# Where the step size of a selective scan is assembled: VectorE, or ScalarE and GpSimd

## The chip, the cores and the metric

The kernel runs on one core of a Trainium2 chip. The metric is the device time of one execution in microseconds (us). The core has four compute engines that this document names: PE (TensorE, matmuls), DVE (VectorE), ACT (ScalarE) and POOL (GpSimd); SP (SyncE) issues the DMA transfers. Each engine takes its own list of instructions in order and waits on semaphores where the list says so.

## The reference

Two layers run one after the other on x of shape 2 x 2048 x 512, all in float32. The first is a selective scan (Mamba) block with adaptive layer norm, the second a linear attention block. The change touches the first layer alone, and in it the step size `dt`:

```python
dt = jax.nn.softplus(einsum('bsr,dr->bsd', dt_r, dt_proj_w) + dt_proj_b)
A = -exp(A_log)                                     # 1024 x 16
def step(h, inp):                                   # over 2048 positions
    dt_t, B_t, C_t, u_t = inp
    dA = exp(dt_t[:, :, None] * A)
    h = h * dA + (dt_t * u_t)[:, :, None] * B_t[:, None, :]
    y = einsum('bdn,bn->bd', h, C_t)
    return (h, y)
y = (y + u * D_param) * silu(z)                     # then out_proj, gate, residual
```

softplus(x) is computed as max(x, 0) + ln(1 + exp(-|x|)). So `dt` is the sum of a rectified part, max(x, 0), and a logarithm.

## The kernel before

The 2 x 2048 positions are cut into 8 chunks (`c`) of 512 positions, and the 1024 channels into 8 blocks (`j`) of 128. One chunk and one block make a unit, `U = 8 * c + j`, so there are 64 units. A unit has 16 slots (`pr`), one for each state index n; `s = 16 * U + pr` counts slots over the program (1024 of them). Two slots form a group `G` (8 per unit), whose 128 x 1024 tile `hb[G % 6]` is one of six buffers. What each engine does for a unit:

- ACT: `softplus(U)` makes `Abs` of the product in PSUM, then `Exp`, then `Ln` in place in the tile `spt`; `exps(s)` writes dA for slot s into one of four PSUM banks (`DA`), three slots ahead of the scan that reads it; `du_copy` copies dt * u into the bank `DU`. ACT also evacuates the projections of the next chunk (`x_evac`, seven ACTIVATEs and sometimes an eighth), applies silu, and copies the end states (`keep_state`). Silu needs another activation table than exp and ln, so each visit to silu has a table load ahead of it and one behind it (L748 by `preload_act_table_set`); silus that share a slot share the two loads.
- DVE: `add(U)` (L933) reads PSUM and `spt` and writes `dt`; `expand(G)` (L943) makes dt * u * B for two state indices; `scan(s)` (L955) runs the recurrence over 512 positions; `y_fin(U)` (L961) multiplies by silu(z).
- POOL: `du(U)` (L1310) makes dt * u; then for each group one multiplication by C of 128 x 1024 (L1339). In the slots of the table `HALF` POOL also adds the two halves of the group (L1344), which saves PE one of two matmuls. POOL adds three taps of the convolution for each of 8 blocks of the next chunk (L1304), and computes the layer norm's small factors (`neg_means` L1297, `rs2` L1288 to L1292), and in chunks 0 and 4 gates the output weights (`gate_w`, L1315).
- PE: sums the 16 states of a unit into PSUM by matmuls with the identity (`nsum`, L299 for the D term, L303 for the groups), and does the projections: `x_mm`, `z_mm` (L250), `proj` (L276), `dt_mm` (L283), `out_mm` (L289).

Waiting between engines: a scan waits for its dA from ACT and its expanded group; ACT's `exps(s)` waits for scan s - 4; POOL's multiplication waits for the group's two scans and, where `kept(U)` holds, for ACT's copy of its end states; `expand(G)` waits until PE has summed group G - 6; `y_fin` of a unit's predecessor waits for its last sum.

The order of the work is written out by hand: at each slot, every engine's loop looks whether `(j, pr)` stands in a table. `AT` holds slots that recur in each unit (`dt`, `soft`, `add`, `du`, `copy`, `yf`), the others (`XMM`, `SILU`, `ZMM`, `STATS`, `RS1`, `SQ`, `RS`, `NORM`, `NTR`, `NEV`, `OUTM`, `OUTA`, `HALF`, `GATE`) slots of a chunk. `XEV` and `TAP` follow from `XMM`. Since each engine takes its list in order, a slot early in one list can come later in time than a later slot of another.

Of the kernel before, what the change touches and what calls it, by code (L numbers as in the profile page):

```python
# [18 lines left out]
def program(nc, A, out):  # L19
# [12 lines left out]
    with ctx:  # L32
        def sem(name):
            return ctx.enter_context(nc.semaphore(name))
# [126 lines left out]
        STATS = {(0, 4): 0, (1, 0): 1}
        RS1 = {(0, 0): 0, (1, 1): 1}
        SQ = {(0, 6): 0, (1, 7): 1}
        RS = {(0, 4): 0, (1, 5): 1}
        NORM = {(0, 8): 0, (1, 10): 1}
        NTR = {(0, 13): 0, (2, 1): 1}
        NEV = {(1, 0): 0, (2, 2): 1}

        OUTM = {(0, 4): 0, (0, 7): 4, (1, 2): 8, (1, 5): 12, (2, 3): 16, (2, 4): 20, (2, 8): 24, (2, 10): 28}
        OUTA = {(0, 9): 0, (1, 9): 1, (2, 8): 2, (3, 0): 3}  # L170
# [1487 lines left out]
```

## Time and profile before

| | |
|---|---|
| time, median of 3 runs | 2452.96 us (2450.15 to 2453.13) |
| profiled execution | 2451.58 us, of which the instructions span 2449.8 us |
| PE busy | 2223.1 us (91%) |
| DVE busy | 2199.2 us (90%) |
| ACT busy | 1618.9 us (66%) |
| POOL busy | 1858.9 us (76%) |
| first scan starts, last scan starts | 81.4 us, 1950.9 us |

The span has three stretches: a start of 81 us, the scan loop of the first layer up to about 1952 us, and the second layer. In the slices of the page DVE stands at 90% or more from the second slice of the scan loop to its end, and POOL and PE at 80% to 90%. The table's shares are means over all three stretches. The chunks are told apart by the start of each one's first scan: 81.4, 322.1, 556.0, 789.2, 1022.0, 1250.4, 1485.5 and 1718.2 us.

### The profile page before, as it was taken

How to read it: one execution, taken by the hardware profiler on the slowest of the kernel's cores; microseconds unless marked ns; L12 is line 12 of the kernel's file. 1: busy time of each engine (PE TensorE's matmuls, PEld its weight loads, DVE VectorE, ACT ScalarE, POOL GpSimd, SP SyncE). 2: the span in 40 equal slices, each digit the busy share in tenths (PEclk: the TensorE clock that was granted, in tenths of full speed). 3: DMA queues.
4: the chain of work that ended last, by engine and by line, in shares of the span. 5: the costliest groups of instructions: out<-in, count | busy, mean ns of one | idle time of the engine just before them, and what ended most of it. 6: DMA issues, size and time to landing. Idle time of an engine off the chain costs nothing. (4 is left out here: it accounts for less than half of the span.)

```text
span 2449.8 us, 24055 instructions
## 1 busy us (share of the span) xinstructions
PE 2223.1 (91%) x6900; PEld 1152.6 (47%) x6900; DVE 2199.2 (90%) x2424; ACT 1618.9 (66%) x3175; POOL 1858.9 (76%) x1205
## 2 busy tenths in 40 slices
PE   8788999899988998898989889988887899999989
PEld 3233334333333433343334333433333389988878
DVE  3799999999999999999999999999999966666656
ACT  3667877777777777777867777777555455466655
POOL 0499989998999899889989998999887722222225
PEclk9899999999999999999999999999998999999999
DMA  5610141123104110412041114112200220011113
GB/s 196 228 57 26 39 156 43 30 97 102 39 26 159 44 35 26 156 52 65 22 177 39 31 47 145 33 30 104 86 31 1 84 76 29 29 57 57 48 52 121
DMA packets 78050, 176.10 MB, mean 72 GB/s; under 512 B 7453, under 2 KB 10781, under 8 KB 77918
## 3 DMA queue, kind: packets, MB, share of 16 engines
q1 hardware_dynamic: 77918, 174.56, 21.5%
q8 instruction: 56, 0.92, 0.2%
q14 instruction: 76, 0.62, 0.1%
HBM read 157.23 MB, written 17.30 MB: 71 GB/s over the span
## 5 line engine op out<-in xcount | busy, mean ns | idle before, releaser
L955 DVE TENSOR_TENSOR_SCAN arena<-ps,arena 128x512 f32<-128x512 f32 x1024 | 1248.9, 1248 | 3.2 <-ACT ps L541 3.2
L1339 POOL TENSOR_TENSOR arena<-arena 128x1024 f32<-128x1024 f32 x512 | 1200.2, 2357 | 65.0 <-ACT arena L541 44.3
L541 ACT ACTIVATE ps<-arena 128x512 f32<-128x512 f32 x1088 | 729.2, 683 | 436.2 <-DVE arena L955 409.8
L303 PE MATMUL ps<-arena,keep 128*128 128x512 f32 x1736 | 840.9, 616 | 104.2 <-POOL arena L1339 57.9
L943 DVE TENSOR_TENSOR arena<-ps,arena 128x1024 f32<-128x1024 f32 x512 | 612.2, 1196 | 22.2 <-PE ps L303 11.6
L303 PEld LDWEIGHTS ps<-arena,keep 128*128 128x128 f32 x1736 | 327.4, 195 | 570.7 <-issue 346.6
L250 PE MATMUL ps<-arena 128*128 128x512 f32 x1024 | 476.2, 610 | 4.6 <-ACT arena L541 3.0
L250 PEld LDWEIGHTS ps<-arena 128*128 128x128 f32 x1024 | 200.7, 197 | 266.4 <-issue 263.2
L541 ACT ACTIVATE arena<-arena 128x2 f32<-128x2 f32 (+2 forms) x597 | 228.8, 386 | 26.4 <-DMA arena<-in_x 10.1
L289 PE MATMUL ps<-arena 128*128 128x512 f32 x512 | 231.3, 592 | 0.0
L1304 POOL TENSOR_TENSOR arena<-arena 128x512 f32<-128x512 f32 x168 | 213.6, 1271 | 9.6 <-ACT arena L541 3.2
L1344 POOL TENSOR_TENSOR arena<-arena 128x512 f32<-128x512 f32 x156 | 197.9, 1268 | 12.2
L541 ACT ACTIVATE arena<-ps,keep 128x509 f32<-128x509 f32 (+3 forms) x240 | 168.6, 703 | 50.3 <-PE ps L250 38.7
L1310 POOL TENSOR_TENSOR arena<-arena 128x512 f32<-128x512 f32 x64 | 81.3, 1271 | 109.9 <-DVE arena L933 109.9
L1357 POOL TENSOR_TENSOR arena_c<-arena_c 128x512 f32<-128x512 f32 x32 | 33.4, 1044 | 167.2 <-DVE arena_c L1104 166.1
L541 ACT ACTIVATE arena<-ps 128x512 f32<-128x512 f32 (+2 forms) x209 | 100.5, 494 | 82.7 <-PE ps L289 27.1
L289 PEld LDWEIGHTS ps<-arena 128*128 128x128 f32 x512 | 97.2, 190 | 122.8 <-issue 122.4
L299 PE MATMUL ps<-arena 128*128 128x512 f32 x128 | 76.1, 679 | 86.0 <-DVE arena L961 85.7
L1271 POOL TENSOR_SCALAR arena_b<-arena_b 128x2 f32<-128x2 f32 x32 | 8.2, 257 | 156.4 <-DVE arena_b L1053 156.4
L541 ACT ACTIVATE arena_b<-ps,keep 128x256 f32<-128x256 f32 x128 | 70.9, 554 | 52.8 <-PE ps L406 43.3
L541 ACT ACTIVATE arena_c<-arena_c 128x256 f32<-128x256 f32 (+3 forms) x112 | 54.9, 493 | 74.6 <-POOL arena_c L1357 47.6
L1064 DVE TENSOR_TENSOR xl<-arena_b,xh 128x256 fp32r<-128x256 f32 x128 | 57.6, 467 | 41.9 <-ACT xh L541 41.1
(138 smaller groups left out, 2567.4 us busy)
## 6 DMA issues: line engine op xcount, KB each, us to landing
arena<-scr_bc SPq DMA_DIRECT2D x128, 512.0 KB, 6.7
arena<-in_inT SPq DMA_DIRECT2D x128, 256.0 KB, 2.7
arena<-in_x SPq DMA_DIRECT2D x17, 512.0 KB, 3.8
scr_x<-arena SPq DMA_DIRECT2D x32, 256.0 KB, 2.0
arena_b<-scr_x SPq DMA_DIRECT2D x16, 512.0 KB, 3.8
arena_c<-scr_x SPq DMA_DIRECT2D x32, 256.0 KB, 2.9
out<-arena_c SPq DMA_DIRECT2D x32, 256.0 KB, 2.0
arena<-in_x SPq DMA_DIRECT2D x30, 256.0 KB, 3.8
```

The costliest lines, as they stand in the source:

```text
L250: last = e.matmul(P, W[:, q, :], xnT[c % 2][:, q, :], start=(q == 0), stop=(q == 3))
L289: e.matmul(P, u[c % 2][:, q, 128 * n:128 * n + 128], wout[:, q, :], start=(c == NCH - 1 and q == 0 or parts and q == 6), stop=(q == 7 or p ...
L299: e.matmul(YP, dg[U % 2], u[c % 2][:, j, :], start=True, stop=False)
L303: last = e.matmul(YP, ident, hb[G % R][:, i, :], start=False, stop=(g == NG - 1 and i == n - 1))
L541: return e.activation(o_, i_, f, **kw)
L943: e.tensor_tensor(hb[G % R], DU.unsqueeze(1).broadcast_to([128, GN, T]), Bt[:, GN * g:GN * g + GN, :], MUL).then_inc(v_tt)
L955: e.tensor_tensor_scan(H, DA[s % 4], H, h0, MUL, ADD).then_inc(v_sc)
L1064: e.tensor_tensor(lo[:, f, :], f_bufs[i % 3], hi[:, f, :].bitcast(f32), SUB).then_inc(v_lo)
L1304: e.tensor_tensor(v, v, tp[:, w, :], ADD).then_inc(g_tap)
L1310: e.tensor_tensor(spt, dt[U % 2], u[c % 2][:, j, :], MUL).then_inc(g_du)
L1339: m_ = e.tensor_tensor(H, H, Ct[:, GN * g:GN * g + GN, :], MUL)
L1344: m_ = e.tensor_tensor(H[:, 0, :], H[:, 0, :], H[:, 1, :], ADD)
```

## The change

In each of the 64 units, DVE's instruction that takes the maximum with zero and adds the logarithm is gone. ACT takes the rectified part from PSUM in a new `Relu` ACTIVATE between `Exp` and `Ln`, and POOL adds `spt` to it in place with a new TENSOR_TENSOR of 128 x 512, ahead of `du`. ACT's exponentials and POOL's `du` now wait for POOL's addition (`g_dt`) where they waited for DVE's (`v_dt`), and the PSUM bank of the product is released by the `Relu`. The tables are written anew; `HALF` has 18 entries in place of 20 a chunk.

```diff
-        AT = {"dt": 4, "soft": 7, "add": 8, "du": 7, "copy": 13, "yf": 7, "proj": (6, 15), "xdbl": (7, 2)}
-        XMM = {(2, 14): 0, (3, 4): 1, (4, 0): 2, (4, 4): 3, (4, 12): 4, (5, 1): 5, (6, 1): 6, (6, 7): 7}
+        AT = {"dt": 5, "soft": 7, "add": 6, "du": 7, "copy": 12, "yf": 6, "proj": (6, 15), "xdbl": (7, 2)}
+        XMM = {(3, 0): 0, (3, 6): 1, (4, 2): 2, (4, 10): 3, (4, 13): 4, (5, 0): 5, (5, 14): 6, (6, 7): 7}
...
-        SILU = {(3, 14): (0, 2), (5, 14): (2, 5), (6, 15): (5, 8)}
+        SILU = {(4, 3): (0, 2), (5, 9): (2, 5), (6, 15): (5, 8)}
...
-        HALF = {0: (5, 7), 1: (1, 3, 7), 2: (0, 2, 3, 4, 5), 3: (0, 2), 4: (3, 4), 5: (3,), 6: (5,), 7: (0, 2, 3, 4)}
+        HALF = {0: (2, 5, 6), 1: (2, 3, 6), 2: (1, 2, 3, 4), 3: (0,), 4: (0,), 5: (), 6: (5,), 7: (0, 3, 4, 5, 7)}
...
-                P = bank(("dt", U), (v_dt, U + 1))
+                P = bank(("dt", U), (a_rl, U + 1))
...
                 e.wait_ge(a_ex, U + 1)
+
+                if U >= 2:
+                    e.wait_ge(g_du, U - 1)
+                act(dt[U % 2], BG[bank_of["dt", U]], ACT.Relu).then_inc(a_rl)
                 act(spt, spt, ACT.Ln, bias=1.0).then_inc(a_ln)
...
-            def add(U):
-                e.wait_ge(a_ln, U + 1)
-                if U >= 2:
-                    e.wait_ge(a_da, 16 * (U - 1))
-                e.scalar_tensor_tensor(dt[U % 2], BG[bank_of["dt", U]], 0.0, spt, MAX, ADD).then_inc(v_dt)
...
+            def add(U):
+                e.wait_ge(a_ln, U + 1)
+                e.tensor_tensor(dt[U % 2], dt[U % 2], spt, ADD).then_inc(g_dt)
+
             def du(U):
                 c, j = divmod(U, 8)
-                e.wait_ge(v_dt, U + 1)
+                e.wait_ge(g_dt, U + 1)
...
+                if U + 1 < NU and pr == AT["add"]:
+                    add(U + 1)
                 if U + 1 < NU and pr == AT["du"]:
                     du(U + 1)
```

On POOL, in unit 0 (chunk 0), before: L1310 is `du`, L1339 the multiplication by C, L1297 `neg_means`, L1288 to L1292 `rs2`, L1344 the halves. The rows begin with `du` of unit 0.

```order
L1310 TENSOR_TENSOR arena<-arena 128x512
L1297 TENSOR_SCALAR arena<-arena 128x2
L1339 TENSOR_TENSOR arena<-arena 128x1024 x2
L1288 TENSOR_SCALAR arena<-arena 128x2
L1290 TENSOR_TENSOR arena<-arena,keep 128x2
L1292 TENSOR_TENSOR arena<-arena 128x2
L1339 TENSOR_TENSOR arena<-arena 128x1024
L1310 TENSOR_TENSOR arena<-arena 128x512
```

The same place now (the lines are those of the changed file: L1303 is the new `add`, L1309 `du`, L1341 the multiplication, L1346 the halves, L1292 `neg_means`, L1283 to L1287 `rs2`).

```order
L1309 TENSOR_TENSOR arena<-arena 128x512
L1341 TENSOR_TENSOR arena<-arena 128x1024 x2
L1292 TENSOR_SCALAR arena<-arena 128x2
L1341 TENSOR_TENSOR arena<-arena 128x1024
L1346 TENSOR_TENSOR arena<-arena 128x512
L1283 TENSOR_SCALAR arena<-arena 128x2
L1285 TENSOR_TENSOR arena<-arena,keep 128x2
L1287 TENSOR_TENSOR arena<-arena 128x2
L1303 TENSOR_TENSOR arena<-arena 128x512
L1309 TENSOR_TENSOR arena<-arena 128x512
```

`neg_means` stood ahead of the unit's first multiplication and stands behind its second. A TENSOR_TENSOR of 128 x 512 is new right ahead of `du`, both still ahead of the unit's fourth multiplication.

On ACT, in unit 5 of a chunk, now: softplus (four rows that alternate between `arena<-ps` and `arena<-arena`), then four rows of exponentials and end states, and a visit to silu with a pair of table loads of its own. Before, that silu of 128 x 1536 stood with the silu of z in slot (5, 14).

```order
L541 ACTIVATE arena<-ps 128x512
L541 ACTIVATE arena<-arena 128x512
L541 ACTIVATE arena<-ps 128x512
L541 ACTIVATE arena<-arena 128x512
L541 ACTIVATE ps<-arena 128x512 x2
L541 ACTIVATE arena<-arena 128x2
L541 ACT_TABLE_LOAD
L541 ACTIVATE arena<-arena 128x1536
L752 ACT_TABLE_LOAD
L541 ACTIVATE ps<-arena 128x512 x2
```

Over the whole program ACT's list has 123 table loads in place of 95 (four more in each of chunks 0 to 6) and 64 more ACTIVATEs `arena<-ps`; POOL's has 64 additions more and 139 halves in place of 156; PE's has 885 matmuls at L303 in place of 868.

## Rows read from the trace of the kernel before

**Rows 1.** Windows, one per chunk: stretch, length, then each engine's busy time
```profile
81.40:322.10 240.70, 208.48 (x466) 81.78 (x467) 230.31 (x216) 170.60 (x347) 221.32 (x127) 0.93 0.27 92
322.10:556.00 233.90, 213.15 (x483) 89.52 (x481) 232.57 (x209) 171.83 (x351) 216.82 (x125) 0.98 0.21 67
556.00:789.20 233.20, 210.96 (x481) 89.33 (x480) 232.57 (x209) 171.18 (x343) 216.14 (x125) 0.98 0.20 68
789.20:1022.00 232.80, 210.35 (x481) 88.94 (x480) 232.53 (x210) 165.41 (x289) 216.00 (x125) 0.99 0.21 68
1022.00:1250.40 228.40, 208.83 (x480) 89.06 (x480) 225.02 (x210) 169.42 (x347) 215.36 (x123) 0.99 0.23 76
1250.40:1485.50 235.10, 214.33 (x490) 91.24 (x489) 232.82 (x210) 173.23 (x352) 220.71 (x127) 0.98 0.22 70
1485.50:1718.20 232.70, 210.54 (x481) 88.70 (x480) 232.49 (x210) 171.44 (x343) 216.02 (x125) 0.99 0.20 66
1718.20:1952.10 233.90, 194.06 (x412) 81.85 (x412) 231.16 (x209) 119.74 (x181) 183.48 (x92) 0.91 0.14 49
```

**Rows 2.** Groups of DVE by line: busy us, mean ns | idle before, releasers
```profile
L955 DVE TENSOR_TENSOR_SCAN arena<-ps,arena 128x512 f32<-128x512 f32 x1024 | 1248.9, 1248 | 3.2 <-ACT ps L541 3.2
L943 DVE TENSOR_TENSOR arena<-ps,arena 128x1024 f32<-128x1024 f32 x512 | 612.2, 1196 | 22.2 <-PE ps L303 11.6 <-ACT ps L541 8.2 <-DMA arena<-scr_bc 2.3
...
L933 DVE SCALAR_TENSOR_TENSOR arena<-ps,arena 128x512 f32<-128x512 f32 x64 | 42.3, 661 | 9.7 <-ACT arena L541 9.7
```

**Rows 3.** Timeline of DVE around one `add`: start, us, instruction
```profile
570.54 1.27 DVE L955 TENSOR_TENSOR_SCAN arena<-ps,arena 128x512 f32<-128x512 f32 x1
571.73 0.66 DVE L933 SCALAR_TENSOR_TENSOR arena<-ps,arena 128x512 f32<-128x512 f32 x1
572.31 1.27 DVE L955 TENSOR_TENSOR_SCAN arena<-ps,arena 128x512 f32<-128x512 f32 x1
```

**Rows 4.** Timeline of DVE at the start of the loop
```profile
76.70 1.22 DVE L943 TENSOR_TENSOR arena<-ps,arena 128x1024 f32<-128x1024 f32 x1 [2.01 <-ACT ps L541]
80.25 1.23 DVE L943 TENSOR_TENSOR arena<-ps,arena 128x1024 f32<-128x1024 f32 x1 [2.33 <-DMA arena<-scr_bc]
```

**Rows 5.** The page's costliest groups: POOL and PE
```profile
L1339 POOL TENSOR_TENSOR arena<-arena 128x1024 f32<-128x1024 f32 x512 | 1200.2, 2357 | 65.0 <-ACT arena L541 44.3
...
L303 PE MATMUL ps<-arena,keep 128*128 128x512 f32 x1736 | 840.9, 616 | 104.2 <-POOL arena L1339 57.9
...
L1344 POOL TENSOR_TENSOR arena<-arena 128x512 f32<-128x512 f32 x156 | 197.9, 1268 | 12.2
...
L1310 POOL TENSOR_TENSOR arena<-arena 128x512 f32<-128x512 f32 x64 | 81.3, 1271 | 109.9 <-DVE arena L933 109.9
```

**Rows 6.** Waits in chunk 2: us in total, times, longest
```profile
POOL arena L1339 <- ACT arena L541: 7.2, 5, 3.6
...
POOL arena L1310 <- DVE arena L933: 3.7, 3, 1.6
...
POOL arena L1297 <- ACT arena L541: 2.9, 1, 2.9
```

**Rows 7.** Waits of POOL in chunk 0
```profile
POOL arena L1297 <- ACT arena L541: 12.0, 1, 12.0
```

**Rows 8.** Timeline of ACT in chunk 2: a visit to silu, and softplus
```profile
666.60 0.69 ACT L541 ACTIVATE ps<-arena 128x512 f32<-128x512 f32 x1 [0.59 <-DVE arena L955]
667.31 1.28 ACT L541 ACT_TABLE_LOAD   x1
668.60 1.08 ACT L541 ACTIVATE arena<-ps 128x512 f32<-128x512 f32 x2
...
683.27 0.59 ACT L541 ACTIVATE arena<-ps 128x512 f32<-128x512 f32 x1
683.89 1.29 ACT L541 ACTIVATE arena<-arena 128x512 f32<-128x512 f32 x2
685.09 0.68 ACT L541 ACTIVATE ps<-arena 128x512 f32<-128x512 f32 x1
```

**Rows 9.** The page's costliest groups: ACT's exponentials
```profile
L541 ACT ACTIVATE ps<-arena 128x512 f32<-128x512 f32 x1088 | 729.2, 683 | 436.2 <-DVE arena L955 409.8
```

More of the change, by code:

```diff
@@ L132, in program @@
             ("ft", "q", "v", "k", "qt", "kt", "kv", "ya", "o"))
-        a_sc, a_A, a_row, a_no, a_xn, a_xh, a_hi, a_tp, a_e0, a_du, a_su, a_xd, a_abs, a_ex, a_ln, a_sz, a_da, a_st, a_dg, a_x1, a_sm, a_sq = (
+        a_sc, a_A, a_row, a_no, a_xn, a_xh, a_hi, a_tp, a_e0, a_du, a_su, a_xd, a_abs, a_ex, a_ln, a_sz, a_da, a_st, a_dg, a_x1, a_sm, a_sq, a_rl = (
             sem("a_" + n) for n in ("sc", "A", "row", "no", "xn", "xh", "hist", "tp", "e0", "du", "su", "xd", "abs", "ex", "ln", "sz",
-                                    "da", "st", "dg", "x1", "sm", "sq"))
+                                    "da", "st", "dg", "x1", "sm", "sq", "rl"))
         a_wh, a_nx, a_f, a_fh, a_qe, a_qT, a_ek, a_E, a_fc = (sem("a_" + n) for n in ("wh", "nx", "f", "hi", "qe", "qT", "ek", "E", "fc"))
-        v_An, v_xe, v_st, v_ag, v_s1, v_tap, v_dt, v_tt, v_sc, v_yf, v_x1, v_xp, v_gb, v_ec, v_a2 = (
-            sem("v_" + n) for n in ("An", "xe", "st", "ag", "s1", "tap", "dt", "tt", "sc", "yf", "x1", "xp",
+        v_An, v_xe, v_st, v_ag, v_s1, v_tap, v_tt, v_sc, v_yf, v_x1, v_xp, v_gb, v_ec, v_a2 = (
+            sem("v_" + n) for n in ("An", "xe", "st", "ag", "s1", "tap", "tt", "sc", "yf", "x1", "xp",
                                     "gb", "ec", "a2"))
@@ L144, in program @@
                                     "att", "y", "o"))
-        g_c, g_r1, g_r2, g_r3, g_rs, g_nm, g_tap, g_du, g_gw, g_m, g_w = (sem("g_" + n) for n in ("c", "r1", "r2", "r3", "rs", "nm", "tap", "du", "gw", "m", "w"))
+        g_c, g_r1, g_r2, g_r3, g_rs, g_nm, g_tap, g_dt, g_du, g_gw, g_m, g_w = (sem("g_" + n) for n in ("c", "r1", "r2", "r3", "rs", "nm", "tap", "dt", "du", "gw", "m", "w"))
         g_att, g_m1, g_mask, g_l1, g_l2, g_lrs, g_q, g_xo = (sem("g_" + n) for n in ("att", "m1", "mask", "l1", "l2", "lrs", "q", "xo"))
@@ L154, in program @@
         XEV = {after(k, 4): i for k, i in XMM.items()}
         TAP = {after(k, (2, 3, 4)[w]): (i, 2 - w) for k, i in XMM.items() for w in range(3)}
-        SILU = {(3, 14): (0, 2), (5, 14): (2, 5), (6, 15): (5, 8)}
-        ZMM = {(1, 8): 1, (1, 10): 2, (3, 8): 1, (3, 10): 2, (5, 7): 1, (5, 11): 2, (7, 11): 1, (7, 12): 2}
+        SILU = {(4, 3): (0, 2), (5, 9): (2, 5), (6, 15): (5, 8)}
+        ZMM = {(1, 8): 1, (1, 10): 2, (3, 8): 1, (3, 11): 2, (5, 6): 1, (5, 10): 2, (7, 10): 1, (7, 13): 2}
@@ L159, in program @@
         ZSILU = {(1, 15): (1, 2), (3, 14): (1, 2), (5, 14): (1, 2), (7, 15): (1, 2)}
[L161 to L170, printed above, removed]
@@ L172, in program @@
-        HALF = {0: (5, 7), 1: (1, 3, 7), 2: (0, 2, 3, 4, 5), 3: (0, 2), 4: (3, 4), 5: (3,), 6: (5,), 7: (0, 2, 3, 4)}
+        STATS = {(0, 1): 0, (1, 2): 1}
+        RS1 = {(0, 3): 0, (1, 0): 1}
+        SQ = {(0, 7): 0, (1, 5): 1}
+        RS = {(0, 5): 0, (1, 5): 1}
+        NORM = {(0, 11): 0, (1, 12): 1}
+        NTR = {(0, 10): 0, (2, 0): 1}
+        NEV = {(0, 15): 0, (2, 1): 1}
+        OUTM = {(0, 9): 0, (0, 10): 4, (0, 14): 8, (1, 4): 12, (2, 2): 16, (2, 7): 20, (2, 10): 24, (2, 12): 28}
@@ L174, in program @@
+        OUTA = {(0, 14): 0, (1, 8): 1, (2, 11): 2, (3, 1): 3}
+        HALF = {0: (2, 5, 6), 1: (2, 3, 6), 2: (1, 2, 3, 4), 3: (0,), 4: (0,), 5: (), 6: (5,), 7: (0, 3, 4, 5, 7)}
         CPART = {after(k, n): (i, n) for i, k in enumerate([(0, 6), (1, 6), (2, 2)]) for n in range(4)}
         CROW, CCOL, CEND = {(0, 11): 0, (1, 11): 1, (2, 7): 2}, {(1, 14): 1, (2, 9): 2}, {(2, 1): 1, (2, 12): 2}
-        GATE = {(1, 8): (0, 0), (1, 12): (0, 1), (2, 0): (0, 2), (2, 4): (0, 3), (38, 14): (1, 0), (39, 3): (1, 1),
-                (39, 7): (1, 2), (39, 13): (1, 3)}
+        GATE = {(1, 10): (0, 0), (2, 15): (0, 1), (3, 13): (0, 2), (4, 14): (0, 3), (39, 1): (1, 0), (39, 6): (1, 1),
+                (39, 14): (1, 2), (39, 15): (1, 3)}
@@ L987, in _ @@
                 taps(i)
-            add(0)
             expand(0)
@@ L998, in _ @@
                 scan(s)
-                if U + 1 < NU and pr == AT["add"]:
-                    add(U + 1)
                 if (U, pr) in ((62, 14), (63, 4)):
@@ L1304, in tap @@
                 e.tensor_tensor(v, v, tp[:, w, :], ADD).then_inc(g_tap)
+            def add(U):
+                e.wait_ge(a_ln, U + 1)
+                e.tensor_tensor(dt[U % 2], dt[U % 2], spt, ADD).then_inc(g_dt)
             def du(U):
                 c, j = divmod(U, 8)
-                e.wait_ge(v_dt, U + 1)
+                e.wait_ge(g_dt, U + 1)
                 e.wait_ge(a_su, su_of(c))
@@ L1319, in _ @@
             rs(1)
+            add(0)
             du(0)
```

## Prediction, made before the changed kernel was run

> **What bounds the kernel now.** I read the windows by chunk first, then the groups by line of DVE and POOL, then the waits of POOL in one chunk, and last the timelines of DVE and ACT around the code that moves. The reader is to see in the windows [rows 1] that the scan loop is bound by DVE: in chunks 1, 2, 3 and 6 it is busy for 232.5 of about 233 us, while PE has 211 to 213, POOL 216 to 217 and ACT 165 to 172. The groups say the same from the other side: 1024 scans sat idle for 3.2 us in total and 512 expansions for 22.2 us [rows 2]. So time taken off DVE in the loop is time off the kernel, as long as no other engine stands close behind. POOL does: it has 216 us of work in a chunk of 233, an idle time of 17 us. That second number decides this case, because the change gives POOL more work and the chunk becomes shorter at the same time. The second layer and the start are as they were, apart from what is said of the first unit below.
>
> **The change part by part.** Sums are made against the profiled execution, 2451.58 us (span 2449.8 us and 1.8 us around it); it lies 1.4 us under the median of the runs, 2452.96 us, so the forecast holds for either within that.
>
> 1. *VectorE's addition goes.* It runs 64 times with a mean of 661 ns [rows 2], but instructions overlap a little: it starts at 571.73 and the next scan at 572.31 [rows 3], so it holds up the line for 0.58 us. 63 of them lie inside the loop: 63 x 0.58 = 36.5 us. In a chunk that is 8 x 0.58 = 4.6 us.
>
> 2. *The first unit.* Here the addition is on the path that starts the loop, and what replaces it is longer: a Relu before the logarithm (0.6 us, from the 0.59 us of Abs over the same shape and source [rows 8]) and 1.27 us of POOL, as du has it [rows 5], in place of 0.66 us. That is 0.6 + 1.27 - 0.66 = 1.2 us later for the first expansion. But the second expansion started only at 80.25, after waiting 2.33 us for the load of B [rows 4]. The delay is shorter than this wait, so I cost it at nothing; without the load as cover it is 1.2 us.
>
> 3. *POOL.* It gets 8 additions a chunk and loses 2 halves (20 entries in the table become 18), at 1.27 us each [rows 5]: +7.6 us a chunk (chunk 4, whose last unit takes no halves, loses 3: +6.4 us). Against the windows [rows 1], with DVE's length shortened by 4.6 us: chunk 2 has 223.7 us of POOL work in 228.6 us, chunks 3 and 6 have 223.6 in 228.1, chunk 1 has 224.4 in 229.3. What is left is 4.5 to 4.9 us of idle where there were 17.1 us (chunk 2). Of those 17.1 us, 7.2 were waits for ACT's copies of the end states, 3.7 for DVE's addition and 2.9 for row sums [rows 6], which leaves 3.3 us for the small gaps between dependent instructions. Those 3.3 us stay. So the waits, 13.8 us, must fall to about 1.3 us, or the chunk gets longer than DVE needs. I expect that most fall, for these waits are those of an engine that has caught up. With less slack POOL runs further behind DVE, and finds the thing it waits for already done. The wait for DVE's addition ends in any case: du stood at slot 7 and waited for an instruction that DVE issued behind scan 8; now POOL waits at slot 6 for ACT's logarithm, which ACT begins once scan 5 has let it issue exponential 9. Behind it in POOL's list stand du and the fourth multiplication, and for these wait ACT's next du_copy and PE's sum. I take 1 us of lost time for each of chunks 1 to 6, 6 us, between 0 and the bounds given under the rivals.
>
> 4. *Chunks 4 and 0.* Chunk 4 had 215.4 us of POOL in 228.4 [rows 1]; now 215.4 + 6.4 + 3.3 = 225.1 us in 228.4 - 4.6 = 223.8, and chunk 5 has 220.7 + 7.6 + 3.3 = 231.6 in 230.5. POOL is the longer one by 1.3 and 1.1 us. Such a shortfall can be carried on as a backlog, for six group buffers lie between the engines, and chunk 7, without taps, has POOL busy only 183.5 of 233.9 us; I add nothing beyond the 1 us each. In chunk 0 POOL waited 12.0 us for row sums at one place [rows 7]; `neg_means` now stands two multiplications later, and the gates are spread from units 1 and 2 to units 1 to 4. Its 10.4 us of DVE idle (240.7 less 230.3) should shrink; I take 2 us as a gain, between 0 and 6.
>
> 5. *ACT.* 64 Relus of 0.6 us are 38 us and 28 more table loads of 1.28 us [rows 8] are 36 us, together 74 us, or 10 us in each of seven chunks (and 5 in the eighth). ACT has 171 of 233 us in chunk 2, and waited for the scans for 409.8 us over the run before exponentials [rows 9], so the sum fits. What counts is the stretch: ACT is three exponentials ahead, some three scans and an expansion or two, about 5 us of cover. Softplus grows from 683.27 to 685.09, 1.8 us, to 2.4 us [rows 8]. Two visits to silu that shared a slot are now apart, each shorter than the joint one, so the longest block does not grow. I cost it at nothing; if the cover is gone, see the rivals.
>
> On the table loads the trace shows one that starts 0.02 us after the exponential before it ends and is followed by the silu 0.01 us after its own 1.28 us [rows 8]. The Trainium skill, ScalarE: Activation LUTs, "What ACT_TABLE_LOAD costs", gives the same 1283 ns but adds a drain of about 1380 ns for each switch; by that rule the 28 loads would be an estimated 75 us of ACT instead of 36, and the rival with ACT would be more likely. This case's trace does not show the drain.
>
> 6. *PE.* 17 more matmuls; 868 at L303 took 840.9 us [rows 5], so 0.97 us each, 2 us a chunk on top of 211 of 233. After the change 213 of 228, not the bound. Releasing the bank by the Relu instead of by DVE behind scan 8 can only help PE. Zero.
>
> Sum: -36.5 (1) + 0 (2) + 6 (3) - 2 (4) + 0 + 0 = -32.5 us. 2451.6 - 32.5 = 2419 us.
>
> **The rivals.**
>
> *A, DVE keeps its whole gain.* POOL's waits vanish, and the idle time of DVE in chunk 0 goes by up to 6 us. Then 2451.6 - 36.5 = 2415 us, down to 2409 us. For it: POOL's waits are short ones, and it had 17 us of idle in every chunk. Against: 4.5 us of slack less 3.3 us of fixed gaps is next to nothing.
>
> *B, POOL is the bound, moderately.* Of 17 us of idle about 6 stay (the gaps and one wait of 3 us). Then chunks 1, 2, 3 and 6 take 230.4, 229.7, 229.6 and 229.6 us, 13 us less than before together; chunks 4 and 5 take 227.8 and 234.3, 1.4 less; chunk 0 keeps the 4.6 us and chunk 7 too. -13 - 1.4 - 9.2 = -24, 2428 us. For it: the totals of rows 1. Against: a backlog can cover part.
>
> POOL takes 1.27 us for what DVE does in 0.66 [rows 2, 5]. The Trainium skill says in the GPSIMD Engine Reference, "Engine selection", that elementwise work belongs on VectorE and is about twice as slow on GpSimd for two inputs; the rows agree. It is a rule against this change, and B and D are what it would come to here.
>
> *C, ACT comes late.* In units 4 and 5 of a chunk the projections, the longer softplus and the lone silu stand close. If DVE waits there 2 to 3 us in each of chunks 0 to 6, 14 to 21 us come back: 2433 to 2440 us. For it: DVE waited for ACT even before, 8.2 and 3.2 us in total [rows 2]. Against: ACT's share of a chunk is only about 80% after the change.
>
> *D, slower.* The waits of POOL [rows 6] are not those of an engine that caught up but are set by ACT, and ACT is later now. Place: POOL's waits for the end states and for the logarithm, at slots 6 and 7 of each unit. A chunk is then POOL's work plus its idle time. Break-even: 233 - 216 - 7.6 = 9 us of idle a chunk; above it the kernel is slower. If 13 us stay, chunks 0 to 6 lengthen by 3.7 us each, 26 us, less 4.6 us for chunk 7: 2473 us. If all 17 stay, 54 - 5: 2500 us. Against it: POOL's waits are few and short (9 in chunk 2, the longest 3.6 us) [rows 6], which is how an engine waits that has caught up, not one that is held back each slot.
>
> That the change doesn't do what it says can be left out: the order of instructions shows no addition on DVE, and no table load between Exp, Relu and Ln.
>
> **How the numbers follow.** Forecast (POOL near full, DVE keeps nearly its pace, 2413 to 2424 us): 0.55. A: 0.13. B: 0.15. C: 0.11. D: 0.06. The range runs from 2411 to 2436 us: it takes in most of A and B and the lower half of C, and leaves out some 5 in 100 below and 11 above. A difference of 0.2% is about what a measurement can tell from none, 5 us; so faster is anything under 2448 us. All cases but D are faster; I keep 0.03 for a mixture that ends within 0.2%, and of D 0.04 for slower, the rest being in between: faster 0.93, same 0.03, slower 0.04.
>
> **What the new profile would show.** For the forecast: no L933-like row on DVE; chunks 1, 2, 3 and 6 at 228 to 230 us with DVE busy for 227 to 228; POOL busy 223 to 224 us in each and its waits for ACT down to a few us. For A: the same with DVE's waits under 0.5 us a chunk. For B: DVE's expansions or its final multiplications wait for PE, and PE for POOL, 1 to 3 us a chunk, with POOL's idle at 5 to 7 us. For C: waits of scans or expansions on ACT's exponentials, above all in units 4 and 5. For D: POOL's idle above 9 us and chunks longer than 233 us. The forecast is wrong at step 1 if DVE's busy time in a chunk doesn't fall by 4.6 us, at step 3 if POOL's work doesn't grow by 7.6 us or its waits stay, and at step 2 if the first scan starts later than 81.4 us.

## The result and the profile after

| | before | after |
|---|---|---|
| median of 4 runs each | 2452.8 us (2450.15 to 2453.13) | 2429.0 us (2427.4 to 2430.5) |
| ratio, 95% interval | | 0.9905 (0.9888 to 0.9922) |
| profiled execution | 2451.58 us | 2427.97 us |
| last scan ends | 1952.1 us | 1926.1 us |

The kernel is 23.8 us faster where 32.5 us were forecast; 2429 us lies inside the range from 2411 to 2436 us. Lines have moved: L953 is the scan, L941 the expansion, L959 `y_fin`, L1341 POOL's multiplication, L1346 the halves, L1299 the taps, L1303 the new addition, L1309 `du`.

These are the windows by chunk of the changed kernel: stretch, length, then busy time (and count) of PE, weight loads, DVE, ACT and POOL, the granted clock, and DMA. They answer to [rows 1].

```profile
81.70:322.70 241.00, 213.46 (x472) 81.32 (x472) 223.81 (x209) 179.82 (x359) 225.72 (x131) 0.94 0.26 91
322.70:552.40 229.70, 211.02 (x484) 88.92 (x484) 228.21 (x202) 179.94 (x363) 224.10 (x131) 0.99 0.21 71
552.40:782.10 229.70, 210.86 (x484) 88.92 (x484) 228.19 (x201) 179.23 (x355) 223.41 (x131) 0.99 0.21 68
782.10:1011.80 229.70, 211.97 (x484) 89.37 (x484) 228.21 (x201) 174.16 (x301) 223.45 (x131) 0.99 0.21 70
1011.80:1238.70 226.90, 209.18 (x485) 88.84 (x486) 221.00 (x201) 177.71 (x359) 223.07 (x129) 1.00 0.23 77
1238.70:1469.80 231.10, 213.79 (x495) 90.10 (x493) 228.46 (x202) 181.43 (x364) 226.46 (x132) 1.00 0.21 70
1469.80:1699.50 229.70, 211.02 (x484) 88.72 (x484) 228.21 (x201) 179.23 (x355) 223.42 (x131) 0.99 0.20 67
1699.50:1926.10 226.60, 197.86 (x422) 83.81 (x423) 226.60 (x202) 122.61 (x189) 191.60 (x98) 0.92 0.14 49
```

DVE's work in chunk 2 fell from 232.57 to 228.19 us, POOL's rose from 216.14 to 223.41. Against before the chunks differ by +0.3, -4.2, -3.5, -3.1, -1.5, -4.0, -3.0 and -7.3 us. Two of these are not what was forecast: chunk 0 gained nothing, chunk 7 gained more than DVE's own 4.6 us. Between the last scan and the second layer's first product 3.2 us more go by, 16.6 in place of 13.4 us (below).

The waits of chunk 2 (us in total, times, longest), which answer to [rows 6]:

```profile
PE ps L303 <- POOL arena L1341: 10.9, 11, 1.7
...
POOL arena L1341 <- ACT arena L541: 2.4, 3, 1.1
...
DVE arena L941 <- PE ps L303: 1.0, 3, 0.4
```

POOL's waits for other engines, 13.8 us before, are down to 2.6 us (with 0.2 us of the taps). PE waits for POOL for 14.6 us (10.9, and 3.7 for the halves) where it was 11.1 us, and DVE waits 1.4 us for PE (1.0, and 0.4 of `y_fin`) where it was 0.2. POOL's idle time in chunks 1, 2, 3 and 6 is 5.6 to 6.3 us. In chunk 0, where DVE waited 2.9 us for PE before, the list shows where the gain went:

```profile
DVE arena L959 <- PE ps L303: 8.4, 2, 5.7
DVE arena L941 <- ACT ps L541: 5.1, 1, 5.1
DVE arena L941 <- PE ps L303: 2.7, 3, 1.3
DVE arena L941 <- DMA arena<-scr_bc: 1.3, 1, 1.3
```

The first row is two waits of `y_fin`, in units 4 and 5, for the last sum of the unit before. The last row, with the start of DVE's timeline, is the cover of the first unit:

```profile
77.96 1.22 DVE L941 TENSOR_TENSOR arena<-ps,arena 128x1024 f32<-128x1024 f32 x1 [13.54 <-ACT ps L541]
80.52 1.23 DVE L941 TENSOR_TENSOR arena<-ps,arena 128x1024 f32<-128x1024 f32 x1 [1.33 <-DMA arena<-scr_bc]
81.66 2.33 DVE L953 TENSOR_TENSOR_SCAN arena<-ps,arena 128x512 f32<-128x512 f32 x2
```

The first expansion starts 1.26 us later than before (1.2 us were forecast), the wait for the load is shorter by 1.0 us [rows 4], and the first scan starts at 81.66 us. In two of the experiments below, whose edits touch nothing ahead of it, the first scan starts at 80.3 and at 84.7 us; so 0.3 us can't be told from none. ACT's list around softplus and the lone silu in unit 5 of chunk 2, which answers to [rows 8]:

```profile
708.07 0.57 ACT L541 ACTIVATE arena<-ps 128x512 f32<-128x512 f32 x1
708.68 0.63 ACT L541 ACTIVATE arena<-arena 128x512 f32<-128x512 f32 x1
709.34 0.60 ACT L541 ACTIVATE arena<-ps 128x512 f32<-128x512 f32 x1
709.83 0.62 ACT L541 ACTIVATE arena<-arena 128x512 f32<-128x512 f32 x1
...
711.78 1.28 ACT L541 ACT_TABLE_LOAD   x1
713.08 1.49 ACT L541 ACTIVATE arena<-arena 128x1536 f32<-128x1536 f32 x1
714.58 1.28 ACT L752 ACT_TABLE_LOAD   x1
```

The Relu is the third row, 0.60 us; softplus takes 2.3 us. The loads cost 1.28 us each and no more, as in the trace of before.

### The profile page after: what moved, and what is told of

Same layout as the page of the kernel before. It is cut to its first block and busy times, and to the rows that moved or that the text cites. A ratio compares the mean times of both kernels' runs of the same rounds, so it can differ in the third digit from the quotient of the medians.

```text
span 2426.2 us, 24198 instructions
## 1 busy us (share of the span) xinstructions
PE 2228.9 (92%) x6934; PEld 1150.8 (47%) x6934; DVE 2163.6 (89%) x2360; ACT 1679.7 (69%) x3267; POOL 1918.9 (79%) x1252
## 5 line engine op out<-in xcount | busy, mean ns | idle before, releaser
L1341 POOL TENSOR_TENSOR arena<-arena 128x1024 f32<-128x1024 f32 x512 | 1198.6, 2357 | 56.2 <-DVE arena L953 32.0
L953 DVE TENSOR_TENSOR_SCAN arena<-ps,arena 128x512 f32<-128x512 f32 x1024 | 1238.4, 1251 | 0.7 <-ACT ps L541 0.6
L303 PE MATMUL ps<-arena,keep 128*128 128x512 f32 x1770 | 858.1, 615 | 119.4 <-POOL arena L1341 89.8
L941 DVE TENSOR_TENSOR arena<-ps,arena 128x1024 f32<-128x1024 f32 x512 | 615.8, 1203 | 32.0 <-ACT ps L541 19.0
L303 PEld LDWEIGHTS ps<-arena,keep 128*128 128x128 f32 x1770 | 331.3, 194 | 600.0 <-issue 341.0
L250 PE MATMUL ps<-arena 128*128 128x512 f32 x1024 | 462.1, 595 | 3.0 <-ACT arena L541 3.0
L250 PEld LDWEIGHTS ps<-arena 128*128 128x128 f32 x1024 | 194.9, 191 | 250.1 <-issue 247.0
L541 ACT ACTIVATE arena<-arena 128x2 f32<-128x2 f32 (+3 forms) x597 | 227.0, 383 | 20.7 <-POOL arena L1299 12.3
L289 PE MATMUL ps<-arena 128*128 128x512 f32 x512 | 231.9, 594 | 0.0
L1299 POOL TENSOR_TENSOR arena<-arena 128x512 f32<-128x512 f32 x168 | 213.4, 1272 | 10.1 <-ACT arena L541 2.0
L541 ACT ACTIVATE arena<-ps 128x512 f32<-128x512 f32 (+2 forms) x273 | 138.8, 517 | 71.7 <-PE ps L250 27.7
L1346 POOL TENSOR_TENSOR arena<-arena 128x512 f32<-128x512 f32 x139 | 177.2, 1275 | 10.9
L289 PEld LDWEIGHTS ps<-arena 128*128 128x128 f32 x512 | 97.8, 191 | 122.9 <-issue 122.4
L1266 POOL TENSOR_SCALAR arena_b<-arena_b 128x2 f32<-128x2 f32 x32 | 8.2, 257 | 154.7 <-DVE arena_b L1048 154.6
L1303 POOL TENSOR_TENSOR arena<-arena 128x512 f32<-128x512 f32 x64 | 81.4, 1272 | 61.3 <-ACT arena L541 61.3
L299 PE MATMUL ps<-arena 128*128 128x512 f32 x128 | 74.5, 665 | 38.5 <-DVE arena L959 37.3
```

Of the source, the lines that this page charges most:

```text
L250: last = e.matmul(P, W[:, q, :], xnT[c % 2][:, q, :], start=(q == 0), stop=(q == 3))
L289: e.matmul(P, u[c % 2][:, q, 128 * n:128 * n + 128], wout[:, q, :], start=(c == NCH - 1 and q == 0 or parts and q == 6), stop=(q == 7 or p ...
L299: e.matmul(YP, dg[U % 2], u[c % 2][:, j, :], start=True, stop=False)
L303: last = e.matmul(YP, ident, hb[G % R][:, i, :], start=False, stop=(g == NG - 1 and i == n - 1))
L541: return e.activation(o_, i_, f, **kw)
L941: e.tensor_tensor(hb[G % R], DU.unsqueeze(1).broadcast_to([128, GN, T]), Bt[:, GN * g:GN * g + GN, :], MUL).then_inc(v_tt)
```

## The experiments

Each is compared with the kernel before on the same chip; the median of the changed kernel itself is 2429.0 us. The medians of the kernel before, beside which they ran, lie between 2450.9 and 2452.8 us, so a difference of 2 us from 2429.0 says little. Unless said otherwise the edit is to the changed kernel.

**Gates of chunk 0 back in their slots.**

```diff
-GATE = {(1, 10): (0, 0), (2, 15): (0, 1), (3, 13): (0, 2), (4, 14): (0, 3), ...
+GATE = {(1, 8): (0, 0), (1, 12): (0, 1), (2, 0): (0, 2), (2, 4): (0, 3), ...
```

> The changed kernel with the four gates of chunk 0 back in slots (1,8), (1,12), (2,0), (2,4). Theory (the gate of 2.4 us in unit 4, among the taps, makes POOL late, and y_fin of units 3 and 4 waits for PE's sum 2.7 and 5.7 us): these two waits shrink to under 3 us together and chunk 0 goes from 241.0 to about 235 to 237 us, total about 2423 to 2425 us. Rival (the early units were as full, the wait only moves): the same us appear in units 2 and 3, chunk 0 stays at 240 to 242 us, total 2428 to 2430 us.

2432.8 us (2430.8 to 2434.2), ratio to before 0.992 (0.9905 to 0.9935). Chunk 0 took 241.4 us, and the waits of DVE are these:

```profile
DVE arena L941 <- ACT ps L541: 6.7, 3, 5.1
DVE arena L959 <- PE ps L303: 5.6, 3, 3.6
DVE arena L941 <- PE ps L303: 2.9, 4, 1.3
```

Units 4 and 5 went from 30.3 and 34.8 us to 28.8 and 29.6, units 2 and 3 from 30.1 and 28.4 to 31.6 and 32.1. The loss moved with the gates and did not go, as the rival said: it isn't a matter of one slot. The total is some 4 us above the changed kernel's, more than the rival had; the profiled loop starts at 84.7 us in place of 81.7, ahead of all that the edit touches, so the rest is not shown to be a price of the gates. The amount of work in chunk 0 was left to test.

**The last unit without its last halves.**

```diff
-halved = lambda U, g: g in HALF[U % 8] and U != 39
+halved = lambda U, g: g in HALF[U % 8] and U != 39 and not (U == 63 and g > 4)
```

> The changed kernel without the halves of groups 5 and 7 in the last unit alone (PE adds two matmuls there). Theory (POOL's last half of 1.27 us and the one before stand ahead of the second layer's first norm factors): from the end of the last scan to the first product of the second layer 16.6 us become 13.5 to 14.5 us, total 2.5 us less, about 2426.5 us. Rival (the second layer waits for the weights' copies and splits, not for POOL): 16 to 17 us as now, total 2429 us.

2427.4 us (2424.7 to 2429.4), ratio to before 0.9898 (0.9882 to 0.9915). The total is not told apart from the changed kernel's, but the place is: the first product starts 12.7 us behind the last scan, where it was 16.6 (13.5 to 14.5 were expected). In the profiled execution chunk 0, which the edit doesn't touch, took 243.4 us in place of 241.0; unit 1 alone took 36.4 in place of 33.9. A single trace's chunk 0 is good to some 2.5 us only. Here is POOL's timeline behind its last multiplications in the changed kernel:

```profile
1924.40 4.66 POOL L1341 TENSOR_TENSOR arena<-arena 128x1024 f32<-128x1024 f32 x2
1929.14 2.12 POOL L1346 TENSOR_TENSOR arena<-arena 128x512 f32<-128x512 f32 x1
1931.35 1.08 POOL L1266 TENSOR_SCALAR arena_b<-arena_b 128x2 f32<-128x2 f32 x1
```

and with the edit, where the last scan ends at 1927.8 us:

```profile
1925.49 4.70 POOL L1341 TENSOR_TENSOR arena<-arena 128x1024 f32<-128x1024 f32 x2 [0.74 <-DVE arena L953]
1930.28 1.08 POOL L1266 TENSOR_SCALAR arena_b<-arena_b 128x2 f32<-128x2 f32 x1
```

L1266 makes the second layer's first norm factors, 5.2 us behind the last scan against 2.5 us. ACT's norm, PE's transposes and the first product hang on it. The new table of halves, made for the 63 units inside, has entries 5 and 7 in the last unit too, where nothing follows that hides them.

**POOL's addition over half of the columns** (the logarithm is left out of the other half).

```diff
-e.tensor_tensor(dt[U % 2], dt[U % 2], spt, ADD).then_inc(g_dt)
+e.tensor_tensor(dt[U % 2][:, 0:256], dt[U % 2][:, 0:256], spt[:, 0:256], ADD).then_inc(g_dt)
```

> The changed kernel with POOL's addition over 256 of the 512 columns (the logarithm is left out of the other half): POOL has 0.6 us less in each unit, 5 us a chunk, PE, ACT and DVE have the same lists. Theory (POOL is full, DVE waits because PE's sums wait for POOL): DVE's waits for PE in chunks 1 to 6 fall from 1.5 to 2.6 us to near nothing, chunks 1, 2, 3 and 6 take 227.5 to 228.3 us in place of 229.7, total 2415 to 2420 us. Rival (PE's own order, a projection ahead of the sum, sets the waits): chunks stay within 0.5 us of 229.7, total 2426 to 2429 us.

2417.2 us (2416.6 to 2422.3), ratio to before 0.9861 (0.9847 to 0.9876). The profiled execution is the one of 2422.3 us; its loop starts at 84.2 us. Chunks 1, 2, 3 and 6 took 228.4, 228.9, 228.5 and 228.4 us, a little more than was expected. The window of chunk 2 and all waits of DVE in it:

```profile
553.00:781.90 228.90, 210.23 (x485) 89.30 (x485) 227.98 (x202) 179.05 (x354) 219.25 (x131) 0.99 0.21 71
```
```profile
DVE arena L941 <- PE ps L303: 0.8, 3, 0.4
```

POOL has 4.2 us less, the chunks are 0.8 to 1.3 us shorter and chunk 5 2.7 us. DVE's waits for PE in these five chunks fall from 8.1 to 2.5 us together, so there they are mostly POOL's lateness. In chunks 4 and 0 they hardly fall, from 5.5 to 4.6 and from 11.1 to 9.9 us. And POOL's own waits for ACT in chunk 2 are back at 5.9 us, from 2.6: given slack again, it catches up and waits. Of what is taken off POOL about a quarter comes back in these chunks, 12 us in the whole run. DVE alone would need 4.6 us less than before a chunk, 228.1 to 228.6 us.

**The tables alone**: the kernel before, with DVE's addition, and the new tables.

```diff
 AT = {"dt": 5, "soft": 7, "add": 8, "du": 7, "copy": 12, "yf": 6, ...     # add stays at 8
 ...                                                                        # all other tables as in the changed kernel
```

> The kernel before (the sum of the step size by DVE) with the new tables: which part of the gain is the tables' alone. Theory (the gain is DVE's 4.66 us a chunk; the tables serve to make room on POOL): no gain by themselves, DVE has 232.1 us a chunk again, chunks 1, 2, 3 and 6 at 232.5 to 234 us, total 2448 to 2455 us. Rival (the tables carry several us of the gain): under 2445 us.

2443.1 us (2441.9 to 2445.5), ratio to before 0.9964 (0.9951 to 0.9977). My theory fell: the tables gain 9 us by themselves. Chunk 2 shows DVE without any idle time:

```profile
551.70:784.20 232.50, 214.29 (x485) 91.05 (x485) 232.50 (x210) 176.72 (x347) 213.90 (x123) 0.97 0.20 68
```

The gain lies in chunks 0 (-3.1 us), 5 (-2.6), 4 (-1.8), 1 (-1.3) and 7 (-3.1), where DVE had waits before; chunks 3 and 6 lost 1.1 us each. POOL still waits here, in chunk 2 for 7.5 us for ACT and for 7.6 us for DVE's addition.

**The instructions alone**: Relu and POOL's addition, with the tables of before.

```diff
 AT = {"dt": 4, "soft": 7, "add": 7, "du": 7, "copy": 13, "yf": 7, ...     # add right ahead of du
 ...                                                                        # all other tables as before
```

> The changed instructions (Relu on ACT, addition on POOL in slot 7 ahead of du) with the tables of before, 20 halves a chunk. The new tables alone gave 9 us, so the instructions with the new tables gave 14 us. Theory (POOL is full; the tables make room on it): POOL has 226.2 us of work a chunk plus 3.3 us of gaps, chunks 1, 2, 3 and 6 at 231 to 234 us with waits of DVE for PE of 3 us or more, total 2436 to 2450 us. Rival (moving the addition is worth its 36 us less small losses whatever the tables): 2420 to 2430 us.

2478.6 us (2476.0 to 2480.8), ratio to before 1.0109 (1.0094 to 1.0124): 26 us slower than before. Both sides of my expectation were too low. The window and the waits of chunk 2:

```profile
565.00:801.20 236.20, 211.64 (x480) 88.62 (x480) 229.15 (x202) 174.65 (x351) 226.06 (x133) 0.99 0.20 66
```
```profile
POOL arena L1341 <- ACT arena L541: 4.1, 2, 3.6
POOL arena L1292 <- ACT arena L541: 1.8, 1, 1.8
```
```profile
DVE arena L941 <- PE ps L303: 5.7, 7, 1.2
```

DVE's work is 3.4 us less than before and its chunk 3.0 us longer. POOL has 10.1 us of idle, above the break-even of 9 us that the prediction gave for case D, and further above the 7 us that the same sum gives for the 20 halves of this run (233.2 - 226.1). The change in the instructions is a loss; with the tables it is a gain. Parts of the tables follow.

**Only the recurring slots new** (on the instructions with old tables: `AT` as in the changed kernel).

> The changed instructions with the tables of before, but the new recurring slots AT (dt 5, add 6, copy 12, yf 6). With all old tables it was 2478.6 us, with all new ones 2429.0. Theory (the crowding of taps, projections and halves in units 3 to 5 makes the loss; POOL is 10 us behind there): the recurring slots alone give under 15 us, total 2463 to 2475 us. Rival (the slots of the addition and of the last multiplication are what counts): over 35 us, total under 2443 us.

2478.9 us (2478.5 to 2481.8), ratio to before 1.0117 (1.0100 to 1.0134): they gain nothing, where the theory had some 4 us at the least and the rival over 35. The slot of the addition isn't what counts on these tables.

**Only the halves new** (on the instructions with old tables: `HALF` as in the changed kernel).

> The changed instructions with the tables of before and the new table of halves alone (18 a chunk, 5 of them in units 3 to 6 cut to 3, more in units 0 and 7). Theory (POOL's load in units 3 to 5 sets the waits): 10 to 25 us less than with all old tables, 2454 to 2468 us. Rival (PE's projections in their old slots set the waits): less than 5 us, 2474 us or more.

2470.8 us (2469.5 to 2473.7), ratio to before 1.0082 (1.0067 to 1.0097): 8 us, between the two expectations.

**The changed kernel with the old tables of the projections.**

```diff
-XMM = {(3, 0): 0, (3, 6): 1, (4, 2): 2, (4, 10): 3, (4, 13): 4, (5, 0): 5, (5, 14): 6, (6, 7): 7}
+XMM = {(2, 14): 0, (3, 4): 1, (4, 0): 2, (4, 4): 3, (4, 12): 4, (5, 1): 5, (6, 1): 6, (6, 7): 7}
 ...                                            # ZMM and SILU too; XEV and TAP follow from XMM
```

> The changed kernel with three tables of before: those of the projections and what follows from them (XMM, ZMM, SILU: when PE multiplies, when ACT evacuates, when POOL adds the taps, when silu runs). The new recurring slots gave nothing on the old tables and the new halves gave 8 us, of 49.5 us between all old and all new. Theory (the crowding of PE, ACT and POOL in units 3 to 5 by the projections is the greater part): total 2445 to 2465 us, DVE waits for PE 5 us or more a chunk in units 3 to 6. Rival (norm, output and gate tables carry the rest): total under 2436 us.

2468.3 us (2467.5 to 2473.0), ratio to before 1.0074 (1.0057 to 1.0090): 39 us slower than with the new ones, and 3 us more than the theory's upper end. In chunk 2:

```profile
562.10:797.10 235.00, 213.37 (x484) 90.26 (x484) 228.28 (x201) 174.13 (x351) 223.31 (x131) 0.97 0.20 67
```
```profile
ACT arena L541 <- PE ps L250: 8.0, 5, 4.5
ACT arena L541 <- PE ps L283: 6.5, 3, 2.6
POOL arena L1341 <- ACT arena L541: 5.7, 4, 2.4
DVE arena L941 <- PE ps L303: 4.4, 5, 1.6
```

POOL's and DVE's work is that of the changed kernel to 0.1 us, and yet the chunk is 5.3 us longer. The first two rows are ACT waiting at the head of its list for projections (L250) and for the product of the step size (L283); they were 1.9 and 1.6 us in the changed kernel. Behind them in ACT's list stand the end states for which POOL waits, 5.7 in place of 2.4 us. So 39 of the 49.6 us between all old and all new tables hang on the slots of the projections, evacuations, taps and silus. That they do so by this chain, PE to ACT to POOL, is read from the waits; PE is also busy for 2.5 us more here, at a granted clock of 0.97 in place of 0.99, and no run tells the two apart.

**PE without 13 of its 110 sums a chunk** (those states are left out of y).

```diff
-n = 1 if halved(U, g) else GN
+n = 1 if halved(U, g) or g in (1, 6) else GN
```

> The changed kernel where PE leaves out the second matmul of groups 1 and 6 of each unit (13 of the 110 sums a chunk, 11 us of PE; the sums of these states are left out). POOL, ACT and DVE have the same lists. Theory (the waits of DVE for PE that remain are POOL's lateness handed on): chunks 1, 2, 3, 6 within 0.5 us of 229.7, total 2425 to 2429 us. Rival (PE's order or load is a cause beside POOL): waits fall to under 0.7 us a chunk, chunk 4 from 226.9 to 223 to 225 us, total 2412 to 2420 us.

2437.6 us (2436.1 to 2439.2), ratio to before 0.9942 (0.9927 to 0.9957). Less work and 9 us slower: neither side had that. Chunks 1, 2, 3 and 6 took 232.0 to 232.6 us. PE's timeline in unit 5 of chunk 2:

```profile
715.45 1.02 PE L303 MATMUL ps<-arena,keep 128*128 128x512 f32 x2
718.68 3.59 PE L303 MATMUL ps<-arena,keep 128*128 128x512 f32 x4 [2.21 <-POOL arena L1341]
```

The same sums in the changed kernel:

```profile
716.10 1.99 PE L303 MATMUL ps<-arena,keep 128*128 128x512 f32 x4 [1.36 <-POOL arena L1341]
```

Four records take 3.59 us behind a wait of 2.21 us for POOL, and 1.99 us behind one of 1.36 us. The wait is longer by 0.85 us because PE came 0.86 us earlier: one sum fewer stands ahead of it (1.02 us for two records, where the changed kernel has 1.88 us for four). The windows around them have the clock in the number behind POOL's count:

```profile
718.80:722.00 3.20, 3.20 (x4) 1.40 (x5) 3.09 (x3) 2.43 (x6) 3.12 (x3) 0.51 0.00 0
722.20:725.50 3.30, 3.30 (x9) 1.44 (x8) 3.12 (x3) 2.83 (x5) 3.30 (x2) 1.00 0.00 0
```

So PE ran at the lower of its two levels, 1.2 GHz, and then at 2.4 GHz. Over chunk 2 the granted clock is 0.96 against 0.99, and PE's busy time fell only from 210.9 to 206.9 us, where sums of 11 us were left out. DVE's timeline over the same stretch shows what it costs:

```profile
722.38 1.22 DVE L941 TENSOR_TENSOR arena<-ps,arena 128x1024 f32<-128x1024 f32 x1 [0.49 <-PE ps L303]
...
727.47 1.23 DVE L941 TENSOR_TENSOR arena<-ps,arena 128x1024 f32<-128x1024 f32 x1 [1.49 <-PE ps L303]
```

Work that left PE came back as a wait for POOL, the clock fell there, and the sums behind it were late: DVE waits 4.0 us for PE in chunk 2, where it was 1.4. The Trainium skill describes such a relapse in TensorE: Matmul & The Clock Gate, "HAM oscillation — how this bites in real kernels", for waits on transfers; here the wait is for POOL.

**Both reliefs together** (the half addition and PE's 13 sums; both parts are left out).

> Both reliefs: POOL's addition over 256 columns, and PE without the second matmul of groups 1 and 6. It gives the length that DVE and ACT set. Theory (DVE is the bound once POOL and PE give way): chunks at 227.5 to 228 us, chunk 4 at 220 to 222, chunk 0 at 230 to 234, total 2400 to 2408 us. Rival (ACT is late in units 4 and 5): waits of DVE for ACT of over 1 us a chunk appear, chunks at 228.5 us or more, total over 2410 us.

2434.9 us (2430.6 to 2440.0), ratio to before 0.9938 (0.9920 to 0.9955). It was to show DVE's own length and does not: DVE waits for PE 2.0 to 6.0 us in each of chunks 1 to 6, and over the run the granted clock is 0.950, the lowest of all kernels here. The total is where the rival had it, but ACT is not the cause: outside chunk 0 DVE does not wait for it.

**Fewer halves**, 16 a chunk, and none late in the last unit.

```diff
-HALF = {0: (2, 5, 6), ... 7: (0, 3, 4, 5, 7)}
+HALF = {0: (2, 6),    ... 7: (0, 3, 5, 7)}
```

> A candidate: the changed kernel with 16 halves a chunk in place of 18 (one less in units 0 and 7), and none behind group 4 in the last unit. POOL has 2.5 us less a chunk, PE 1.7 us more. Theory (POOL is what is full): chunks 1, 2, 3, 6 at 228.6 to 229.4, the second layer's first product 13 us behind the last scan, total 2419 to 2425 us. Rival (PE is as full): chunks at 229.7 or longer, total 2427 us or more.

2434.4 us (2426.2 to 2435.4), ratio to before 0.9921 (0.9902 to 0.9941). Not a gain, and the rival's numbers: chunks 1 to 4 took 230.4 to 232.3 us, 1.5 to 3.5 us more than in the changed kernel. The window of chunk 2:

```profile
556.30:787.50 231.20, 212.43 (x489) 89.89 (x488) 228.40 (x202) 179.25 (x355) 221.17 (x129) 0.99 0.21 69
```

POOL has 2.2 us less than in the changed kernel and PE 1.6 us more, at the same clock; DVE waits 2.7 us for PE in place of 1.4. What is taken off POOL here is given to PE, unlike in the half addition, and as the waits read, PE's sums come later for it. So it isn't POOL alone that stands close behind DVE. Chunks 5 and 6 took 230.9 and 229.7 us, no more than in the changed kernel, and one of the four executions took 2426.2 us against 2434 to 2435; why they differ so stays open.

**Fewer halves in chunk 0 alone**, in the units of its gates, and none late in the last unit.

```diff
-halved = lambda U, g: g in HALF[U % 8] and U != 39
+halved = lambda U, g: g in HALF[U % 8] and U not in (2, 3, 4, 39) and not (U == 63 and g > 4)
```

> A candidate: the changed kernel with no halves in units 2, 3 and 4 of chunk 0 (6 fewer, 7.6 us less of POOL, 5 us more of PE, where POOL has the gates as well) and none behind group 4 of the last unit. Theory (chunk 0 is held by POOL's work, the gates added to taps): chunk 0 from 241 to 243 us to 235 to 238 us, with the second layer's first product 13 us behind the last scan; total 2419 to 2424 us. Rival (PE or its clock holds chunk 0): chunk 0 at 240 us or more, total 2426 to 2428 us.

2422.7 us (2420.5 to 2425.5), ratio to before 0.9885 (0.9870 to 0.9899), the fastest that computes everything: 6.3 us under the changed kernel by the medians, 4.4 us if each is taken against the kernel before beside it; the intervals of the two ratios overlap a little.

```profile
81.60:320.10 238.50, 215.50 (x484) 83.37 (x484) 222.90 (x209) 179.35 (x359) 218.26 (x125) 0.96 0.25 92
```

Chunk 0 is 2.5 us shorter than in the changed kernel, with POOL's 225.7 us down to 218.3, and unit 1 takes 33.9 us in both, so this is no matter of that unit. The theory had the sign and less than half of the size; DVE still waits 9.9 us for PE there (11.1 in the changed kernel). The boundary gives its 3.9 us once more (12.7 us).

## Why the prediction was right in sign and 9 us too far

The sum was -32.5 us, the profiled executions differ by -23.6.

1. *DVE's addition, -36.5 us.* Right. 4.3 to 4.4 us of busy time are gone in each of chunks 1, 2, 3 and 6, 232.5 to 228.2, 0.2 to 0.3 us short of the 4.6.
2. *First unit, 0.* Right to 0.3 us, as the load of B covers 1.0 of 1.26 us. By its own sign, a first scan later than 81.4 us, this step would be wrong; the start differs by more than that between executions.
3. *POOL, +1 us for each of chunks 1 to 6.* Right in size, and in part in mechanism. POOL's work rose by 7.3 us (7.6 forecast), its waits for others fell from 13.8 to 2.6 us (1.3 wanted). Against DVE's 4.6 us chunks 1, 2, 3 and 6 lost 0.4, 1.1, 1.5 and 1.6 us, 4.6 together where 4 were set; chunk 5 lost 0.6. The half addition shows that most of this is POOL, and it bears out the reason too, that waits vanish because POOL has less slack: with 4.2 us less work its waits for ACT came back, 5.9 us in place of 2.6. But less slack is not enough. With the old tables POOL has 2.7 us more work than with the new, and its waits for ACT stay at 6.7 us, of 10.3 before. With the old projections alone they are 8.4 us (5.7 and 2.7), with ACT itself waiting for PE; and the tables without the new instructions leave 7.5 us. Both were needed. The prediction set the price of the tables at nothing beyond the halves and gates. With the old instructions they are worth 9 us, with the new ones 50. No term of the sum had looked at this; that the tables fit the change, and kept it from case D, was luck for the forecast.
4. *Chunks 4 and 0.* The step that failed. Chunk 0 was to be 6.6 us shorter and is 0.3 us longer: 6.9 of the 8.9 us. The 2 us for the vanished wait of 12.0 us [rows 7] were wrong. It lies at the start of the loop, before and after: POOL's `du` ends at 76.0 us (77.3 now), the first two scans end at 83.7 us (84.0 now), and POOL multiplies from 88.20 us (87.14 now). So at most 4.5 us could be gained there and 1.1 us was. It no longer waits for row sums, but for ACT's copy of the end states, which now stands behind them and the silus in ACT's list:

```profile
76.03 1.26 POOL L1309 TENSOR_TENSOR arena<-arena 128x512 f32<-128x512 f32 x1
87.14 4.66 POOL L1341 TENSOR_TENSOR arena<-arena 128x1024 f32<-128x1024 f32 x2 [9.84 <-ACT arena L541]
```

The copy in the trace of before, and now:

```profile
84.38 0.19 ACT L541 ACTIVATE arena<-arena 128x2 f32<-128x2 f32 x1
```
```profile
86.87 0.19 ACT L541 ACTIVATE arena<-arena 128x2 f32<-128x2 f32 x1
```

The 4.6 us of DVE's addition were counted for chunk 0 without the sum that the prediction made for chunks 1 to 6; by it POOL would have 232 us in 236 there (221.3 + 7.6 + 3.3), and POOL's wait at the start of the loop, of which 5.4 us lie inside the chunk, takes up more than the rest. DVE waits 11.1 us for PE there, where it was 2.9. By unit, 0 to 2 are 5.8 us shorter than before, and 4 and 5, where gates meet taps, are 5.5 us longer. Moving the gates back moved the loss, taking six halves away got 2.5 us of it back; what holds the rest is not shown, and 2.5 us is also what chunk 0 differs by between executions. In chunk 4 the backlog did not pass: -1.5 us in place of -3.6. There DVE waits 5.5 us for PE, and leaving out half of POOL's addition takes only 0.9 us off that; the cause stays open.
5. *ACT, 0.* Right. Its work is 8 us more in chunk 2 (10 forecast), and DVE waits for it only in chunk 0 and for 0.3 us in chunk 4. Case C did not occur.
6. *PE, 0.* On load, 211 us as before where 213 were forecast. But PE is not as far off as its share says. Two sums more a chunk in place of two halves lengthened chunks 1 to 4 by 1.5 to 3.5 us, and 13 sums fewer lengthened chunks 1, 2, 3 and 6 by 2.3 to 2.9 us at a lower clock, which the prediction left out. So PE is not the bound, and yet late sums reach DVE.

Two terms were missing, and nearly cancel by luck: the waits of DVE in chunk 7 before, 2.7 us more gained (the tables alone gain 3.1 us there), and the boundary to the second layer, 3.2 us lost.

Of the cases, 2429 us is above the 2413 to 2424 us of the forecast, which had 0.55; the time is that of B, POOL moderately the bound, which had 0.15. B's figures are met in chunks 1, 2, 3 and 6: it had 230.4, 229.7, 229.6 and 229.6 us and 5 to 7 us of idle on POOL, and they took 229.7 us each with 5.6 to 6.3. Elsewhere it is right by cancelling: it had chunks 4 and 5 at 227.8 and 234.3 us (226.9 and 231.1 measured), kept DVE's 4.6 us in chunk 0 (4.9 us too much) and in chunk 7 (2.7 too little). D was set at 0.06 because POOL's waits looked like those of an engine that caught up. Without the tables D is what happens.

## What to carry to other kernels

When work is moved off the bound onto an engine with a few per cent of slack, the slack must be read chunk by chunk, and the start and the end of the loop apart. The move and the placement of everything else are one change: here the instructions alone cost 26 us, the placement alone gave 9, both together 24. Before relieving an engine further, look who gets its work (16 halves in place of 18 loaded PE and cost 5 us) and whether its next wait lowers its clock, and look at table entries that also hold in the last unit, where the next stage stands behind them.
